# Expert stage: the down weights are issued by ScalarE on its own queue instead of SyncE

## The reference

```
T = 2048 tokens, E = 64 experts, K = 8 of them per token, F = 192, CAP = 128
logits = xf @ router_w.T;  scores = softmax(logits);  topk_w, topk_idx = top_k(scores, K)
buf[expert * CAP + pos] = xf[token]          # at most CAP tokens for an expert
gate = einsum('ech,ehf->ecf', xb, w_gate);   up = einsum('ech,ehf->ecf', xb, w_up)
hmid = silu(gate) * up
yb   = einsum('ecf,efh->ech', hmid, w_down)
out[token] += yb[slot] * topk_w
```

## Time and profile before

| | |
|---|---|
| median of 3 runs | 3058.5 us |
| lowest, highest | 3056.04, 3063.08 us |
| profiled execution | 3060.83 us, its span 3059.0 us |
| granted TensorE clock, mean | 0.943 |
| PE busy | 2639.5 us (86%) |
| DVE, ACT, POOL busy | 57%, 42%, 26% |
| expert stage | from about 2628 us to the end |
| loads in the expert stage | 51 of gate, 51 of up, 51 of down, 384.0 KB each |

### The profile page before, as it was taken

One profiled execution on the slowest core, in us unless ns is written; L12 is line 12 of the kernel. 1 busy time (PEld: TensorE's weight loads), 2 busy tenths in 40 slices (PEclk: granted clock), 3 DMA queues, 4 the chain that ended last, 5 costly groups with the idle time before them and its releaser, 6 DMA issues. The chain is left out here.

```text
span 3059.0 us, 48349 instructions
## 1 busy us (share of the span) xinstructions
PE 2639.5 (86%) x17099; PEld 2107.4 (69%) x17099; DVE 1738.9 (57%) x3888; ACT 1272.6 (42%) x3385; POOL 805.6 (26%) x825
## 2 busy tenths in 40 slices
PE   3888988579999599999699999999999972588885
PEld 2555655479999488887588888888888862345452
DVE  4767676674433566666466666666666647422221
ACT  1666666222222344444355555555555531121111
POOL 2222311000000255555222222222222210244443
PEclk8999998789999799999799999999999986799998
DMA  3010100330000555555712421421331138499986
GB/s 124 12 46 19 46 19 19 111 95 15 29 28 8 173 182 187 192 186 186 222 50 56 134 54 43 124 67 40 91 109 42 36 102 291 127 290 290 272 219 113
DMA packets 227055, 340.10 MB, mean 111 GB/s; under 512 B 24512, under 2 KB 110976, under 8 KB 226304
## 3 DMA queue, kind: packets, MB, share of 16 engines
q1 hardware_dynamic: 211904, 297.14, 31.3%
q0 software_dynamic: 14912, 39.85, 5.8%
HBM read 230.60 MB, written 110.53 MB: 112 GB/s over the span
## 5 line engine op out<-in xcount | busy, mean ns | idle before, releaser
L1706 POOL TENSOR_SCALAR a_prob<-a_prob,a_rinv 128x640 f32<-128x640 f32 (+3 forms) x256 | 252.4, 986 | 770.2 <-DVE a_rinv L1861 770.2
L1851 DVE TENSOR_REDUCE a_mx<-a_s_ps 128x1 f32<-128x640 f32 (+3 forms) x256 | 262.3, 1025 | 274.2 <-PE a_s_ps L1775 267.9
L1727 ACT ACTIVATE a_probT<-a_t_ps 128x512 fp32r<-128x512 f32 (+3 forms) x512 | 237.2, 515 | 369.4 <-PE a_t_ps L1783 369.4
L1867 DVE TENSOR_TENSOR a_probT<-a_t_ps,a_probT 128x512 fp32r<-128x512 f32 (+3 forms) x512 | 276.7, 582 | 47.2 <-ACT a_probT L1727 47.1
L1718 ACT ACTIVATE a_prob<-a_s_ps,a_nb,a_rs 128x640 f32<-128x640 f32 (+3 forms) x256 | 267.7, 1046 | 0.0
L137 PE MATMUL a_o_ps<-a_probT,a_v 128*128 128x256 f32 x832 | 245.4, 295 | 0.0
L139 PE MATMUL a_o_ps<-a_probT,a_v 128*128 128x256 f32 x832 | 235.1, 283 | 0.0
L138 PE MATMUL a_o_ps<-a_probT,a_v 128*128 128x256 f32 x832 | 235.1, 283 | 0.0
L1783 PE MATMUL a_t_ps<-a_ident,a_prob 128*128 128x128 f32 x1664 | 225.9, 274 | 8.5 <-DVE a_probT L1867 5.9
L137 PE MATMUL f_bank<-f_xT,f_gu 128*128 128x256 f32 x704 | 204.9, 291 | 19.1 <-DVE f_gu L1114 19.1
L554 PE MATMUL a_bank<-a_ident,a_prob 128*128 128x128 f32 x1024 | 168.2, 291 | 58.9 <-ACT a_prob L445 33.8
(11 more groups left out here) (299 smaller groups left out, 6737.9 us busy)
## 6 DMA issues: line engine op xcount, KB each, us to landing
m_wgu<-in_w_gate SPq DMA_DIRECT2D x64, 384.0 KB, 3.9
m_wgu<-in_w_up SPq DMA_DIRECT2D x64, 384.0 KB, 5.4
m_wd<-in_w_down SPq DMA_DIRECT2D x64, 384.0 KB, 7.6
l_q_hi<-p_turned SPq DMA_DIRECT2D x64, 256.0 KB, 2.7
l_q_lo<-p_turned SPq DMA_DIRECT2D x64, 256.0 KB, 2.5
a_qT<-l_q_hi SPq DMA_DIRECT2D x64, 256.0 KB, 3.6
a_qT<-l_q_lo SPq DMA_DIRECT2D x64, 256.0 KB, 4.2
l_v_hi<-p_vs SPq DMA_DIRECT2D x32, 256.0 KB, 2.7
```

The costliest lines, as they stand in the source:

```text
L1706: pool.tensor_scalar(prob[:, k % 4, 0:w], prob[:, k % 4, 0:w], rinv[:, k % 4:k % 4 + 1], 1.0, ALU.mult, ALU.mult).then_inc(s["weighted"], 1)
L1727: act.activation(probT[0][:, pair % 2, i * 4:i * 4 + n, k % 2], t_ps[i][:, 0:n * P].rearrange("p (m n) -> p m n", n=P), ACT.Copy).then_inc ...
L1851: step(dve.tensor_reduce(mx[:, k % 4:k % 4 + 1], s_ps[:, k % 2, 0:w], AX.X, ALU.max))
L1867: dve.tensor_tensor(probT[1][:, pair % 2, i * 4:i * 4 + n, k % 2], t_ps[i][:, 0:n * P].rearrange("p (m n) -> p m n", n=P), probT[0][:, pai ...
```

## The change

Loading is split in two functions. `load_gate_up` stays with SP in the expert stage, under the same wait. `load_down` is called in ACT's loop, behind `copy_h(e - 1)` and ahead of `copy_x(e + 1)`, for the buffer of expert e-3; it increments the same semaphore `w_loaded[u]`. There are 51 such calls, for experts 13 to 63, in ACT's iterations 3 to 53. The 13 experts loaded ahead in `route` are still loaded by SP, all three weights.

```diff
-def experts(nc, table, out, second, slots, wgu, wd, w_loaded, load):
+def experts(nc, table, out, second, slots, wgu, wd, w_loaded, load_gate_up, load_down):
...
             def _(sp):
                 for e in range(RING_E, E):
                     sp.wait_ge(s["y_done"], e - RING_E + 1)
-                    load(sp, e)
+                    load_gate_up(sp, e)
...
                 for e in range(E + 1):
                     if e:
                         copy_h(e - 1)
+                    if e >= 3 and e - 3 + RING_E < E:
+                        load_down(act, e - 3 + RING_E)
                     if e < E:
                         copy_x(e + 1)
...
-        def load(eng, e):
+        def load_gate_up(eng, e):
             u = e % RING_E
             for i in range(2):
                 eng.dma_start(wgu[:, u, i], gu_src[i][e]).then_inc(w_loaded[u], 16)
+
+        def load_down(eng, e):
+            u = e % RING_E
             eng.dma_start(wd[:, u], d_src[e]).then_inc(w_loaded[u], 16)
+
+        def load(eng, e):
+            load_gate_up(eng, e)
+            load_down(eng, e)
+
```

More of the change, by code:

```diff
@@ L2361, in load @@
                 eng.dma_start(wgu[:, u, i], gu_src[i][e]).then_inc(w_loaded[u], 16)
+        def load_down(eng, e):
+            u = e % RING_E
             eng.dma_start(wd[:, u], d_src[e]).then_inc(w_loaded[u], 16)
+        def load(eng, e):
+            load_gate_up(eng, e)
+            load_down(eng, e)
         route(nc, d, x_in, table, out, slots, load, second)
-        experts(nc, table, out, second, slots, wgu, wd, w_loaded, load)
+        experts(nc, table, out, second, slots, wgu, wd, w_loaded, load_gate_up, load_down)
         st.clear()
```

## The result

The changed kernel takes 3066.73 us (median of 6 runs, 3065.47 to 3073.62), the kernel before beside it 3055.68 us (3051.53 to 3063.08). The ratio is 1.0038, 95% interval [1.0023, 1.0053]: slower by 11 us. A second set of runs gave 1.0051 [1.0033, 1.0069]. That set also tells what a ratio is worth: the kernel before, timed once more as if it were another kernel, came out at 1.0016 [1.0003, 1.0029]. Beside this control, in the same set, the changed kernel is 10 us slower (medians 3072.12 and 3061.94). A ratio within about 0.0016 of 1 is therefore read as no difference here. My forecast was no change, 3058 us; the range 3042 to 3080 holds the time, the direction was missed.

A forecast was written before the change was run, and what follows sets the result against it. The prediction took the expert stage to be bound by full DMA engines, the gather contending with weight loads. Its terms, 0 + 0 + 0 + 0 − 1 = −1 us, gave 3057.5 from the median 3058.5; forecast 3058, no change, range 3042 to 3080.

The forecast's parts named there:

- What bounds the stage: Expert stage during weight loads: gather contending with weights sets the loop, 6.15 us an expert against TensorE's 5.25, 45 us.
- The section on spare DMA time: DMA engines in the expert stage: full, 6.1 us an expert against a pace of 6.15; only serving order can change.
- SP's part: 51 down-weight issues leave SP, which is idle most of the time with nothing awaited behind them: value 0.
- ACT's part: 51 issues of 0.43 us between ACT's copies of h and x, with up to 1.54 us free: price 0.
- the added condition: ACT waits for nothing new; the down weight, issued later, is not needed for another 11 experts: value 0.
- The transfers: Down-weight bytes beside the gather in each period: same time and same collision as before, 0; bounds −11 and −45 us.
- The rival with the third queue: ACT's queue takes turns from the gather in the expert stage: +11 us, 3069, at worst 3091; chance 0.23.
- The clock: TensorE's clock drops after long gather waits; an episode is worth a few us of either sign; one more, chance 0.02.
- The ends of the stage: Down loads shift by 1.5 experts, their missing thirds running in the quiet regime: −1.3 us, taken as −1.

The follow-up runs named there:

- e5_ahead6: The kernel before with six gather buffers instead of four (AHEAD = 6), all loads still on SP: 3013.41 us, ratio 0.9869.
- e1_sp_late: The changed kernel with the down weight back on SP's queue, still issued 2.8 us after the down matmuls: 3070.88 us, ratio 1.0038 to the kernel before.
- e7_sp_next: Against the kernel before: SP issues the down weight one expert later, at the same +0.9 us behind gate and up: ratio 1.0002.
- e9_sp_later: Against the kernel before: all loads on SP, the down weight issued 4.7 us after the down matmuls, when the next x is turned: ratio 1.0065.
- e6_ahead6_act: The changed kernel with six gather buffers instead of four: 3016.28 us, ratio 0.9866 to the kernel before.
- e8_sp_mid: Against the kernel before: SP issues all three loads of an expert together, 2.8 us after the down matmuls: 3137.36 us, ratio 1.0248.

## Why the prediction was wrong, point by point

**What bounds the stage** was half right. The gather's latency in the loop and TensorE's wait for it, 45 us to be had, were read rightly: e5_ahead6 got back 42 of them. The section on spare DMA time was wrong. It added up packet times by queue to 6.1 us an expert and set them equal to the pace of 6.15. But packet times overlap, so their sum is no floor. In e5_ahead6 the loads' packets again take 49.4% of 390 us, 3.78 us an expert, and the share reads 1.06 while the pace falls. By the estimate above, two queues would have allowed 5.7 us an expert, not 6.1.

**SP's part, ACT's part, the added condition**: right. SP's issues were free; ACT's took 0.32 us, less than the 0.43 assumed, and lay beside the copy of h, not behind it: so its moment was +2.8 and not the +3.2 of the prediction. e1_sp_late has none of them and the whole loss.

**The transfers: this step failed.** I took 0, "for place and bytes are the same". The bytes were the same; the place was not. The down weight went from +0.9 to +2.8 us and its landing from +8.2 to +8.5 in one profile, to +6.8 in the other, but on SP's queue it had been behind gate and up, which use the time before the gather's own issue at +3.5. Moved, it leaves a lighter stretch before the gather and a heavier one beside it. I judged the collision by whether it was there, not by how much of each load fell on which side of the gather's issue. By experiment, all on SP's queue: +0.9 costs nothing (e7_sp_next, 1.0002), +2.8 costs 1.0038, +4.7 costs 1.0065, and the whole burst at +2.8 costs 1.0248. The gather on the chain goes the same way: 6.09, 6.39, 6.75 and 8.01 us. For the changed kernel it went from 6.21 to 6.53 and 6.49 us; by my estimate 0.3 us in each of 25 turns is 8 of the 11 us. The term that I put at 0 is this one. That the cost comes from sharing the engines packet by packet is the natural reading, but no view here shows single packets; the runs show the dependence on the moment, not what happens inside the engines.

**The rival with the third queue** had the size, 3069 us, and the wrong mechanism. Its +11 us was worked out from turns between queues; the third queue alone gave 1.0017 and 1.0007 at SP's moment, and e1_sp_late and e9_sp_later have a loss without it. That the size agreed was luck. The Trainium skill, "DMA: Bandwidth & Descriptors", section "Queues, rings and completion order", says that an engine goes round between the rows that have work; the runs neither show nor deny that, but the ratios with a third row at the early moment (1.0017 and 1.0007) are below those with one load moved by 2 us (1.0038, 1.0051 and 1.0038). The same page's section "Rules for kernel authors" says that spreading DMAs over SP, ACT and GpSimd does not help bandwidth. In e6_ahead6_act it went with 319 instead of 299 GB/s, the moment being changed as well, and did not help the time.

**The clock** was put at a few us of either sign. It can add to a loss: in e8_sp_mid a down matmul took 733 ns in the mean from 2660 to 2950, against 631 before. At the size of this change it is not the cause: the changed kernel has 659 and 642 ns against 631 and 634, but e1_sp_late has 627 and e9_sp_later 617, at granted clocks of 0.98 in the stretch, and both are slower than before.

**The ends of the stage** were worth −1 in my sum. From the last gate load to the end of the span the profile after has 101.9 us and that before 105.1, but the control has 101.7 without the change, so no gain in the tail is shown. Between the first and the last load 19 us were lost in the first pair of profiles (326.83 against 307.58) and 7 in the second.

## What to carry to other kernels

When a latency loop runs beside bulk loads, look at the moment at which the bulk is issued before you look at the queue that carries it; here it mattered more. Start it as far as possible ahead of the transfer that the loop waits for, and never together with it. Before tuning that moment, give the loop another buffer or two: here two more gather buffers were worth 42 us, and after them neither queue nor moment mattered. A DMA share near 1 is no proof that the engines are full; ask whether the same bytes would still go through if the waiting ended. And profile a kernel twice before you read a few us out of one profile: here two profiles of one kernel differ by 16 us in the stage.

## What the runs showed of the hardware

- The DMA share of 0.98 at 281 GB/s was not a ceiling: 1.06 at 302 GB/s with two queues, and 1.04 at 319 GB/s with three.
- With two queues at 302 GB/s SP's issues of loads stretched from 0.34 to 0.47 us to as much as 6.3 us, and the loads went at 6.07 us an expert while TensorE took 5.25.
- A DMA issue on ACT took 0.32 us and started together with the ACTIVATE ahead of it in program order (both at 2700.12).
- Moving a burst of 1.125 MB by 2.8 us, so that it starts with the gather, cost 72 us in 51 experts, 1.4 us each, the lower clock included.
- The same kernel against itself came out at 1.0016 with an interval that excludes 1. Differences of this size need a control in the same set of runs.
